# A written order for attention's last unit, an earlier load of the first sums' weights, and statistics one tile a chunk

## The reference, cut to what matters

```python
x = x + _L0_attn_a_ref(_layernorm(x), ...)
x = x + _L0_ffn_ref(_layernorm(x), ...)
x = x + _L0_attn_b_ref(_layernorm(x), ...)      # scores + alibi bias, softmax, @ v, @ Wo.T
x = x + _L0_ffn_ref(_layernorm(x), ...)         # w_eff = w * (su @ sv)
# _L0_ffn_ref: a = linear(x, gate); b = linear(x, up); d = silu(a) * b; return linear(d, down)
```

## Time and profile before

| | before |
|---|---|
| median of 3 runs | 2451.26 us (2450.16 to 2452.91) |
| the profiled execution, its own time | 2452.54 us |
| its span | 2451.2 us |
| mean granted TensorE clock | 0.987 |
| PE busy | 2376.9 us, 97% |
| DVE, ACT, POOL busy | 1647.0, 1191.9, 797.8 us |

### The profile page before, as it was taken

The page is one execution under the profiler, slowest core; times in us unless marked ns, Lnnn a source line. Parts: engine busy times, 40 slices in busy tenths (PEclk is TensorE's granted clock), DMA queues, the critical chain, the costliest instruction groups (busy, mean ns, idle before and its releaser), DMA issues. The chain is left out here.

```text
span 2451.2 us, 40849 instructions
## 1 busy us (share of the span) xinstructions
PE 2376.9 (97%) x12810; PEld 2028.4 (83%) x12810; DVE 1647.0 (67%) x3961; ACT 1191.9 (49%) x3788; POOL 797.8 (33%) x1204
## 2 busy tenths in 40 slices
PE   6799999999989999999999999999999979999999
PEld 4577777888878888989889888889998867888887
DVE  7666664534267877777787777777777776565553
ACT  6433332233256666666666666666666552222222
POOL 4540343212144344444443444444334340001000
PEclk9899999999999999999999999999999989999999
DMA  4234558998751534535446345353252214555554
GB/s 139 101 124 174 193 210 293 348 350 328 276 204 39 231 120 161 213 146 197 155 175 231 122 161 212 148 195 154 96 202 90 99 65 176 195 208 186 193 193 155
DMA packets 86579, 444.85 MB, mean 181 GB/s; under 512 B 9496, under 2 KB 16664, under 8 KB 66656
## 3 DMA queue, kind: packets, MB, share of 16 engines
q1 hardware_dynamic: 85008, 440.78, 48.2%
q10 hardware_dynamic: 1360, 1.46, 0.2%
HBM read 342.59 MB, written 99.61 MB: 180 GB/s over the span
## 5 line engine op out<-in xcount | busy, mean ns | idle before, releaser
L773 PE MATMUL psum<-qw,xs 128*128 128x384 f32 x2688 | 511.7, 340 | 2.7 <-issue 1.7
L773 PEld LDWEIGHTS psum<-qw,xs 128*128 128x128 f32 x2688 | 461.7, 188 | 4.2 <-issue 2.9
L2411 POOL TENSOR_SCALAR prob<-prob,rsum 128x128 f32<-128x128 f32 (+1 forms) x512 | 227.8, 460 | 625.3 <-DVE rsum L2509 620.3
L2357 ACT ACTIVATE prob<-biased,nmax 128x256 f32<-128x256 f32 (+1 forms) x512 | 227.5, 447 | 135.9 <-DVE nmax L2499 135.7
L773 PE MATMUL psum<-wo_h,oT_h 128*128 128x512 f32 x512 | 212.9, 416 | 0.1
L773 PE MATMUL psum<-wo_l,oT_h 128*128 128x512 f32 x512 | 200.9, 392 | 0.0
L773 PE MATMUL psum<-wo_h,oT_l 128*128 128x512 f32 x512 | 200.4, 391 | 0.0
L2318 ACT ACTIVATE squares<-cc 128x128 f32<-128x128 f32 x512 | 152.6, 302 | 54.9 <-DVE cc L2457 52.2
L2484 DVE TENSOR_TENSOR cc<-cc,rr 128x512 f32<-128x512 f32 x64 | 96.9, 1514 | 101.5 <-POOL rr L2401 101.5
L2401 POOL TENSOR_TENSOR rr<-ss,mneg_half 128x6 f32<-128x6 f32 (+1 forms) x128 | 150.6, 1176 | 10.7
L773 PE MATMUL psum<-xT0h,wgu 128*128 128x512 f32 x448 | 153.1, 401 | 0.0
(11 more groups left out here) (338 smaller groups left out, 5863.5 us busy)
## 6 DMA issues: line engine op xcount, KB each, us to landing
xs<-weff_x SPq DMA_DIRECT2D x62, 1792.0 KB, 7.7
wgu<-weff_gu SPq DMA_DIRECT2D x42, 1024.0 KB, 7.6
weff_q<-q_parts SPq DMA_DIRECT2D x56, 768.0 KB, 4.0
qw<-weff_q SPq DMA_DIRECT2D x56, 768.0 KB, 8.2
wD<-weff_dn SPq DMA_DIRECT2D x56, 512.0 KB, 4.8
wS<-weff_s SPq DMA_DIRECT2D x28, 1024.0 KB, 6.9
wdn<-weff_dn SPq DMA_DIRECT2D x42, 512.0 KB, 4.1
weff_gu<-wgu SPq DMA_DIRECT2D x14, 1024.0 KB, 4.2
```

The costliest lines, as they stand in the source:

```text
L773: ins = pe.matmul(out_ap, stat[a], mov[b], start=start and n == 0, stop=stop and n == last)
L2357: act.activation(prob[:, b, lo:hi], biased[:, b % 2, lo:hi], ACT.Exp, bias=nmax[:, b, t:t + 1], scale=-1.0, accum_out=esum[:, b, t:t + 1]) ...
L2411: pool.tensor_scalar(prob[:, b, lo:hi], prob[:, b, lo:hi], rsum[:, b, t:t + 1], 1.0, ALU.mult, ALU.mult).then_inc(prob_done, 1)
```

## The change

1. `closing` and its scheduler call go. The order of the last unit and of the eight rows is written out for each engine in `LAST_UNIT`. The instructions are the same, except that some that `Steps` had put behind each other are now apart.
2. The ring of `xf` and `xt` has three places instead of four. Only one of them lies over `later`.
3. The first of the two `wS` buffers moves ahead of `later` in the memory map, and its load for chunk 0 is issued within attention's last unit, as soon as all projections are over (`loads0` at the end of SP's list), instead of after attention's end. The other loads still wait for attention's end.
4. The statistics of the last eight tiles are made after `u2` of chunks 1 to 8, one tile a chunk.

```diff
-            norm_steps(second, 3, T, [("u2", 0, 0)] * TPB)
+            norm_steps(second, 3, T, [("u2", 1 + (T - 2) * TPB + j, 0) for j in range(TPB)])
...
+        wS = [sb3("wS0", [P, 2, 8 * P], F32R)]
         later = sb3("later", [P, IC, BLK])
...
-        more = over("more", [P, 4, 2 * KC * P], F32, "later")
-        ROWS_RING = (TPB, 2)
+        more = over("more", [P, 2, 2 * KC * P], F32, "later")
+        ROWS_RING = (3, 2)
...
-        wS = [sb3(f"wS{r}", [P, 2, 8 * P], F32R) for r in range(2)]
+        wS.append(sb3("wS1", [P, 2, 8 * P], F32R))
...
-        closing = Steps({})
...
-        order_closing = closing.ordered()
+        LAST_UNIT = {
+            "pe": "sc0 fxT0 fxT4 sc1 sc2 sc3 fxT5 fxT1 pT0 pT1 fxT6 fxT2 at0 pT2 pT3 fxT7 fxT3 at1 outa0 out0 outa1 "
+                   "out1",
...
+            "pool": "pcomb0 norm0 norm1 norm2 pcomb1 norm3 pcomb2 pcomb3",
+            "sp": "loads0",
+        }
         for e in order2:
-            order2[e] += order_closing[e]
+            for name in LAST_UNIT[e].split():
+                order2[e].append((name[:-1], UNITS - 1 if name[:-1] in ATTENDING else 0, int(name[-1])))
...
+                elif what == "loads":
+                    over_projections(sp, g)
+                    load_sums(g)
...
         def sp_phase3():
             phase2_over(sp)
-            load_sums(0)
             load_products(1)
```

More of the change, by code:

```diff
@@ L1825, in hybrid_block @@
         xt = sb3("xt", [P, 2, 4, KC // 2, P])
+        wS = [sb3("wS0", [P, 2, 8 * P], F32R)]
         later = sb3("later", [P, IC, BLK])
         xr = over("xr", [P, 2, DM], F32, "up2")
-        more = over("more", [P, 4, 2 * KC * P], F32, "later")
-        ROWS_RING = (TPB, 2)
[L1832 to L1835, removed]
-        wS = [sb3(f"wS{r}", [P, 2, 8 * P], F32R) for r in range(2)]
+        more = over("more", [P, 2, 2 * KC * P], F32, "later")
+        ROWS_RING = (3, 2)
+        xf_ring = [xf[:, r, :, :, :] for r in range(2)] + [more[:, 0, :].rearrange("p (h k c) -> p h k c", h=2, k=KC)]
+        xt_ring = [xt[:, r, :, :, :] for r in range(2)] + [more[:, 1, :].rearrange("p (t k c) -> p t k c", t=4, k=KC // 2)]
+        rows_end = cursor["phase3"] - IC * BLK * 4 + 2 * 2 * KC * P * 4
+        wS.append(sb3("wS1", [P, 2, 8 * P], F32R))
         wA = [sb3(f"wA{r}", [P, 2, 6 * P], F32R, "phase3" if r else "ffn2_head") for r in range(2)]
```

## The result

| | before | changed |
|---|---|---|
| median | 2451.42 us (6 runs, 2449.87 to 2455.47) | 2439.34 us (6 runs, 2434.62 to 2444.50) |
| ratio, 95% interval | | 0.9949 [0.9935, 0.9964] |
| the profiled execution's span | 2451.2 us | 2439.7 us |

The changed kernel is 12.1 us faster (by the interval 8.8 to 15.9). The forecast was 8.9 faster.

The account below looks back on a forecast made before the run. TensorE was taken as the bound, so only its waits or low-clock time could be given back; in the last unit GpSimd was the long pole. 6.2 + 1.3 + 1.4 = 8.9 off 2451.26 gave 2442.4 us, range 2438.6 to 2446.6.

Parts of the forecast that it names:

- The start of chunk 0: Second feed-forward's first chunk after attention's last unit: begins at 2012.4 instead of 2018.58, 6.2 us earlier.
- the walk: Step-by-step timing of the last unit's written order from `sc0`: GpSimd as long pole ends at 2010.0, chunk 0 begins 2012.4.
- Rival A: GpSimd's meetings cost little, TensorE's own work ends last: chunk 0 starts 8.9 earlier without waiting, 2439.7 us; chance 0.17.
- The meetings: VectorE steps beside GpSimd's `pcomb` in the last unit: 0.87 for each of three `plo`, 0.8 for four `frow`.
- The reading of the earlier trace: `plo` and the addition beside it both lengthen at once (1.54 and 1.61), neither by the other's whole length.
- The clock: Chunk 0's first product runs at the full clock level after a shorter TensorE wait: 1.3 us given back.
- The statistics: Moved out of chunk 0, they remove TensorE's 1.38 wait for `u3`: 1.4 us; one pair a chunk stays covered.
- The load: `wS` for chunk 0 issued early: gives nothing by itself but is needed; chunk 1's loads cause no wait.
- rival C: Chunk 1 waits for its loads behind `oadd1`, if they take 3 longer: 6.9 us faster, 2444.4; chance 0.05.
- The sum: Start of chunk 0, clock and statistics together: 6.2 + 1.3 + 1.4 = 8.9 us faster, median 2442.4.

## Why the prediction was right

- **The start of chunk 0** (the first term, 6.2). It came 24.2 after the first `frow`; the walk had 2012.4 − 1988.5 = 23.9. Against before that is 5.9. Rival A, whose 2439.7 the first median matches, had the start 8.9 earlier and no wait before it; neither came about, so that match is chance. The first `pcomb` began 2.6 after the first `frow` (walk: 2.4), GpSimd had no gap, and the last wait was for `plo3` (1.5, forecast 1.9). That the first product stands at 2008.71, and not between 2011.5 and 2013, is the unit's earlier beginning (1984.54) and no part of the walk. The walk's two conditions are shown apart: with the transposes late the unit is 7.9 longer, with the norms first 3.8.
- **The meetings** (2.6 for three `plo`, 0.8 for four `frow`). Measured on GpSimd: norm3 2.05 against 0.99 undisturbed, and additions of 1.78 and 1.71 against 0.74, 3.1 in all for the three `plo`. Beside the `frow` two additions of 0.92 and 0.80 against 0.73 give under 0.3. GpSimd's 19.1 us in the unit are 3.4 over the undisturbed 12.1 + 3.6, just as forecast, but by luck: one term was too small and the other too large. The table's unit says 2.0 for what the `plo` meetings cost.
- **The reading of the earlier trace rows**, that both engines are lengthened at once, did not hold. The row shows a chain of two waits. The addition ahead of the one shown had begun before the `plo`:

```profile
2204.46 0.73 POOL L2147 TENSOR_TENSOR xt<-xf 128x256 f32<-128x256 f32 x1
```

It ended at 2205.19. The `plo` from 2204.74 was held up by it (1.54 in place of 1.21) and ended at 2206.28, and the next addition was held up by the `plo` and ended 0.60 later, at 2206.88. In the first trace of the changed kernel no addition in the unit had more than 0.03 left when a `plo` began, and VectorE's three `plo` took 1.21, undisturbed; the two additions beside them ended 0.60 behind them. So an engine loses what is left of the other's step when it comes to its own, here about 1.0 and never the whole 1.21. This agrees with the Trainium skill's rule (page "SBUF — State Buffer", section "Who interferes with whom": the one that comes second is blocked, the other runs on) better than the prediction granted. Which one comes second can't always be told from the recorded starts: norm3's first instruction began 0.23 ahead of `plo0` and was the one held up.
- **The clock** (1.3). The first product took 1.46 in place of 2.69, 1.2 less. With a wait of 1.5 the level was 1.00 there, with waits of 6.8 to 7.6 it was 0.50.
- **The statistics** (1.4). The wait of 1.38 goes with them and returns with them, and chunks 1 to 8 have no new wait.
- **The load** (0, but needed). Shown by its return: 4.3 of waiting and 3.1 to 3.5 of clock. For chunk 1, the loads that stand behind `oadd1` came barely in time: the weight load of its product 6 waited 0.4 for `wS` (2019.81), so that rival C was closer than its 0.05 said. The prediction's own numbers had `wA` arrive at 2022.5 for a use at 2022.0, which is not "No wait"; `wA` was there in time.
- **The sum.** 5.9 + 1.2 + 1.4 = 8.5 measured part by part against 8.9 forecast. The measured medians are 12.1 and 10.9 faster, with intervals from 8.8 and from 7.6 on. The 2.4 to 3.6 us between stay open: no trace has more than 0.8 of them in the unit or behind it (waits for `wD` aside), and the scatter ahead of the unit (10 us over twelve traces) is larger. That the small `wD` wait differs by 2 between two traces of the same kernel (2.5 and 0.5) is part of that scatter.

One reading behind the walk did not hold: that GpSimd, being full, is by itself what bounds the unit. Taking a step off it gave nothing, and taking 3.1 of lengthening off it gave 2.0.

## What to carry to other kernels

Where the last piece of one phase and the preparation of the next share four engines, look for the step whose place in one list makes all others late; here the transposes of two rows, put back behind the output products, cost the whole gain, and the engine that looked full was only one of several. When the start is brought forward, every load that was hidden under the old wait has to be moved with it: the one that gives nothing by itself was worth 5.3 to 6.5 us in the new order. And a gain of 0.5% on a program that scatters by 0.2% is read from the length of the changed stage in the trace, not from one median.

## What the runs showed of the hardware that had not been expected

After the wait of 4.3 us for `wS`, the granted clock was at its lower level for some 6 us of uninterrupted matmuls (from 2020.28 to about 2026.3), against 2.8 us after the wait of 7.2 in the kernel before. A shorter wait was followed by a longer stretch of work at 1.2 GHz. The windows (columns as in the earlier trace rows) show what differed. In the kernel before, the level had fallen by the time the last transposes ended (2011.36), so the whole wait passed at the lower level:

```profile
2011.50:2018.00 6.50, 0.00 (x0) 0.00 (x0) 3.43 (x4) 3.41 (x6) 4.34 (x5) 0.50 1.01 375
```

With the load back, the first product had run at the full level, the level was still full for most of the wait, and it fell only between 2019 and 2020, just before the work resumed:

```profile
2014.50:2019.00 4.50, 1.47 (x6) 0.86 (x5) 0.34 (x1) 1.88 (x2) 0.00 (x0) 1.00 0.67 220
```

In these two traces, what the clock cost went with when the level fell, and not with the length of the wait alone.
